# Two gated 3x3 convolutions on one core: the 18 products of the first 12 steps whose results nobody reads are left out

## The chip, the cores and the metric

The kernel runs on one core of a Trainium2 chip. The metric is the device time of one execution in microseconds (us). Several executions are timed; the median stands for the kernel. One execution was also profiled, and all rows below are of that one.

## The reference, cut to what matters

A residual block with two 3x3 convolutions over x of shape (16, 64, 56, 56) in float32. Each convolution is split by input channels: the first 16 channels give yp, the other 48 give yr, and yr is scaled by a gate made of yp.

```python
def qconv_cg(x, w, theta):
    base = x.shape[1] // 4
    yp = conv3x3(x[:, :base], w[:, :base])
    yr = conv3x3(x[:, base:], w[:, base:])
    d = sigmoid(2.0 * (yp - theta[None, :, None, None]))
    return yp + d * yr

h = relu(bn(qconv_cg(x, w_a, theta_a), gamma_a, beta_a, mean_a, var_a))
h = bn(qconv_cg(h, w_b, theta_b), gamma_b, beta_b, mean_b, var_b)
return relu(x + h)
```

## The kernel before, in words

**Rows and tiles.** The 64 input channels are four groups (g = 0 to 3) of 16. Two image rows of opposite parity lie beside each other in the partitions, so a group has 32 partitions and a product of TensorE contracts over the 32 rows of one group. TensorE's array thus works as four row tiles, one for each group; products on different row tiles run beside each other. Group 0 makes yp, groups 1 to 3 add up yr. x and the intermediate h are split into a high and a low part (x_hi, x_lo, h_hi, h_lo), the weights too (w_hi, w_lo); a block of output rows needs 18 products per group: high by high, high by low and low by high weight parts in turn, six taps each (`unit`, lines 502 to 514; the product itself is line 511).

**Steps.** The products are emitted in steps. In a step each group that has work emits one product, in the order g = 1, 2, 3, 0 (lines 519 to 525). `begins` (line 516) says at which step a group starts its next block: group 1 at step 18 times the visit, group 2 six steps later, group 3 twelve steps later (`OFFSET`, line 32); group 0 is without its offset for its first three visits (`EARLY`). So in steps 0 to 5 only groups 1 and 0 have a block, in steps 6 to 11 groups 1, 2 and 0, and from step 12 on all four. Which block a group takes at which visit is set by `TURNS` (line 30): group 1 starts with block 0, group 2 with block 1, group 3 with block 2, and group 0 with block 0.

**The products nobody reads.** Lines 538 to 545 put, at the head of each of the first 12 steps, one more product on the row tile of every group of 2 and 3 that has no block yet: group 2 in steps 0 to 5, group 3 in steps 0 to 11, 18 in all. Each takes weights and x of its group's partitions with 398 columns (`SPARE`) and writes PSUM bank 1 (group 2) or bank 2 (group 3) with start and stop set. The first real product of group 2 in bank 1, and of group 3 in bank 2, starts its sum anew. At step 0 they wait for the same two semaphores (`xhi0_ready`, `whi_ready`) that the first real product waits for at lines 552 and 553.

**What TensorE does ahead of step 0.** Seven products of 128 rows and 512 columns on zeros (line 465, `WARM`), then 12 transposes that bring the weights of the first convolution into their layout (line 457). ScalarE copies the transposed weights to w_hi (line 601), VectorE makes w_lo (line 730).

**What ends the waits near the change.** Block 0's x_hi is cast by VectorE (line 773). Block 1's x_hi is made by ScalarE (`split_hi`, line 621) behind the copies of w_hi and a table load with a first use of Sqrt (line 631). Group 2's first product, at step 6, waits for it (line 555, `xhi_ready`); TensorE takes its products in order, so what is emitted behind that wait waits too.

```python
            for g in (1, 2, 3, 0):
                for visit in range(TOTAL):
                    for u in range(UNITS):
                        steps.setdefault(begins(g, visit) + u, []).append((g, visit, u))
```

Of the kernel before, what the change touches and what calls it, by code (L numbers as in the profile page):

```python
# [23 lines left out]
ROWS = 2 * GR  # L24
BLK, BLK_B = 8, 9
SHORT, SHORT_PAIRS = 7, 2
# [5 lines left out]
OFFSET = (6, 0, 6, 12)  # L32
# [8 lines left out]
def gated_conv_pair_kernel(nc, x, w_a, theta_a, gamma_a, beta_a, mean_a, var_a,  # L41
# [5 lines left out]
    PITCH = W + 1  # L47
# [110 lines left out]
    with ExitStack() as ctx:  # L158
# [64 lines left out]
        whi_ready = sem("whi_ready")  # L223
# [224 lines left out]
        @block.tensor  # L448
        def _(pe):
            def weights(k, c, bank):  # L450

                pe.wait_ge(wpad_ready, 4 + 2 * k + 1 + c)
                pe.wait_ge(wpad_odd_ready, 2 * k + 1 + c)
                for dx in range(TAPS):
                    to = psum[:, bank, dx * P:(dx + 1) * P].rearrange("p (c q) -> p q c", q=2)
                    for mq in range(2):
                        last = pe.transpose(  # L457
                            to[:, mq], w_pad[k][:, 2 * c - mq + 1, dx].rearrange("o i q -> o (i q)"),
                            ident[:])
                last.then_inc(wt_ready, 1)  # L460


            pe.wait_ge(zeros_ready, 1)
            for n in range(WARM):
                mm = pe.matmul(psum[:, 0, :], h_lo[:, 0:P], h_lo[:, 0:BANK], start=True, stop=True)
            mm.then_inc(warm_done, 1)
            pe.wait_ge(ident_ready, 2)
            for c in range(2):
                weights(0, c, 6 + c)
            pe.wait_ge(warm_done, 1)  # L470

            def moving(blk, part, c, dx, g):

                kind, n = blk
                rows = slice(g * ROWS, (g + 1) * ROWS)
                back = 1 - leading(blk)
                if kind == "a":
                    tile = (x_hi, x_lo)[part]
                    parts = a_slots[n]
                    img, s, k = parts[0]  # L480
                    at = back + (s + c) * PITCH + dx
                    if len(parts) == 1:
                        return tile[rows, img % XH_IMGS, at:at + k * PITCH - back]
                    return tile[rows, img % XH_IMGS:img % XH_IMGS + 2, at:at + k * PITCH]
                if kind == "e":
                    return (e_hi, e_lo)[part][rows, c, dx:dx + EDGE * PITCH]
                img, s, k = b_slots(n)
                at = back + ((img % H_IMGS) * SLOTS + s - 1 + c) * PITCH + dx
                return (h_hi, h_lo)[part][rows, at:at + k * PITCH - back]

            def sums(bank, blk):

                kind, n = blk
                to = psum[:, bank, 0:slots_of(blk) * PITCH - 1 + leading(blk)]
                if kind == "a" and len(a_slots[n]) == 2:
                    return to.rearrange("p (i w) -> p i w", i=2)
                return to

            UNITS = 2 * TAPS * 3
            SPARE = SHORT * PITCH - 1  # L500

            def unit(g, b, u):

                kind, n = blk = order[b]
                hi, lo = {"a": (w_hi[0], w_lo[0]), "b": (w_hi[1], w_lo[1]), "e": (w_edge_hi, w_edge_lo)}[kind]
                kind3, tap = divmod(u, 2 * TAPS)
                part, w = ((0, hi), (0, lo), (1, hi))[kind3]
                c, dx = divmod(tap, TAPS)
                bank = YR_BANKS + b % YP_BANKS if g == 0 else b % YR_BANKS
                alone = g == 0  # L510
                return pe.matmul(sums(bank, blk), w[g * ROWS:(g + 1) * ROWS, tap],  # L511
                                 moving(blk, part, c, dx, g),
                                 start=(u == 0 and (alone or g == bank_groups(b)[0])),
                                 stop=(u == UNITS - 1 and (alone or g == bank_groups(b)[-1])))

            def begins(g, visit):
                return UNITS * visit + (0 if g == 0 and visit < EARLY else OFFSET[g])

            steps = {}
# [5 lines that stand above are left out]
            for step in sorted(steps):  # L525
                if step == 24:
                    pe.wait_ge(prmdup_ready, 2)
                    pe.transpose(psum[:, 7, 0:10], prm_dup[:].rearrange("n c q -> n (c q)"),
                                 ident[0:10, 0:10]).then_inc(prmT_ready, 1)
                if step in W_STEPS:  # L530

                    c = W_STEPS.index(step)
                    if c:
                        pe.wait_ge(wlo_ready, 3)
                    else:
                        pe.wait_ge(rvar_ready, 1)
                    weights(1, c, W_BANK)
                for g in (2, 3):
                    if step < OFFSET[g]:

                        if step == 0:
                            pe.wait_ge(xhi0_ready, 1)
                            pe.wait_ge(whi_ready, 1)
                        pe.matmul(psum[:, g - 1, 0:SPARE], w_hi[0][g * ROWS:(g + 1) * ROWS, 0],  # L544
                                  x_hi[g * ROWS:(g + 1) * ROWS, 0, 1:1 + SPARE], start=True, stop=True)
                for g, visit, u in steps[step]:
                    b = visited(g, visit)
                    kind, n = blk = order[b]
                    if u == 0 and g == bank_groups(b)[0]:
                        if kind == "a":  # L550
                            if n == 0:
                                pe.wait_ge(xhi0_ready, 1)
                                pe.wait_ge(whi_ready, 1)
                            else:
                                pe.wait_ge(xhi_ready, chunks_needed(n) - 1)
                        else:
                            pe.wait_ge(hhi_ready, a_needed((kind, n)))
                            if (kind, n) == ("b", 0):
                                pe.wait_ge(hpads_zero, 4)
                            if kind == "e":  # L560
                                pe.wait_ge(edges_ready, 2 * (edge_sources.index(a_needed(blk) - 1) + 1))
                                pe.wait_ge(wedge_ready, 4)
                        if b >= YR_BANKS:
                            pe.wait_ge(gated_ready, b - YR_BANKS + 1)
                    if b == 0 and g == 1 and u == TAPS:
                        pe.wait_ge(whi_ready, 2)
                    if b == 0 and g == 1 and u == 2 * TAPS:
                        pe.wait_ge(wlo_ready, 2)
                    if u == 4 * TAPS and g == bank_groups(b)[0]:
                        if kind == "a":  # L570
                            pe.wait_ge(xlo_ready, chunks_needed(n))
                        else:
                            pe.wait_ge(hlo_ready, 2 * a_needed((kind, n)))
                    if u == 0 and group_before(g, b):

                        pe.wait_ge(visit_done[group_before(g, b)], visits(group_before(g, b), b))
                    if g == 0 and u == 0 and b >= YP_BANKS:

                        pe.wait_ge(gate_ready, b - YP_BANKS + 1)
                        was, m = order[b - YP_BANKS]  # L580
                        if was == "a":
                            pe.wait_ge(za_ready, m + 1)
                        else:
                            pe.wait_ge(zb_ready, second_of[was, m] + 1)

                    if g == 0 and u == 0 and b == 1:
                        pe.wait_ge(wlo_ready, 2)
                    if g == 0 and u == 0 and b == 2:
                        pe.wait_ge(rvar_ready, 1)
                    if u == 0 and b == 4 and g == bank_groups(b)[0]:  # L590
                        pe.wait_ge(whi_ready, 4)
                        pe.wait_ge(wlo_ready, 4)
                    mm = unit(g, b, u)
                    if u == UNITS - 1:
                        mm.then_inc(visit_done[g], 1)
# [292 lines left out]
```

## Time and profile before

| what | value |
|---|---|
| median of 3 runs | 440.07 us (439.25 to 441.33) |
| the profiled execution, its own time | 439.4 us |
| its span, first to last instruction | 437.5 us |
| TensorE busy (matmul) | 427.3 us, 98% of the span, 7826 products |
| ScalarE, VectorE, GpSimd busy | 197.2, 245.1 and 32.2 us |
| mean granted TensorE clock | 0.994 |

The span is 1.9 us shorter than the execution's own time; that remainder lies around the span and belongs to the launch. Busy times are shares of the whole span and say nothing about one stage: the start, in which the change lies, is read from a timeline. The profile models the end of a product, so the distance between two starts on one row tile says more than the duration of one product.

### The profile page before, as it was taken

The page shows a single profiled execution, that of the slowest core. Times are in us where ns is not written, and L with a number is a line of the kernel's source. Part 1 is how long each engine was busy: PE and PEld are TensorE (multiplying, and loading weights), DVE is VectorE, ACT ScalarE, POOL GpSimd, SP SyncE. Part 2 cuts the span into 40 slices and gives each one's busy share as a digit, 9 for nine tenths or more (in the row PEclk, how much of TensorE's full clock was granted, in tenths as well). Part 3 has the DMA queues.
Part 4 walks back from the last instruction along what each step waited for, and adds up shares of the span by engine and source line. Part 5 has one row for each costly group of instructions (what it writes and reads, how often), then busy time and mean ns, then how long its engine had stood idle before and what let it go on. Part 6 is the DMA issues. An engine that isn't in the chain of part 4 may idle for free.

```text
span 437.5 us, 17328 instructions
## 1 busy us (share of the span) xinstructions
PE 427.3 (98%) x7826; PEld 423.9 (97%) x7826; DVE 245.1 (56%) x414; ACT 197.2 (45%) x340; POOL 32.2 (7%) x82
## 2 busy tenths in 40 slices
PE   7999999999999999999999999999999999999992
PEld 6999999999999999999999999999999999999992
DVE  6566546744754862574475476366457457536624
ACT  6755344534534652453353453354345344424223
POOL 6221000000000100000000000011000000000001
PEclk9999999999999999999999999999999999999997
DMA  8920026142426110410523241161622422012044
GB/s 170 190 62 4 3 49 122 35 92 51 88 37 124 25 27 2 99 43 11 124 50 75 49 98 41 37 120 26 121 49 51 76 49 49 3 27 51 14 86 92
DMA packets 119530, 27.57 MB, mean 63 GB/s; under 512 B 119328, under 2 KB 119328, under 8 KB 119456
## 3 DMA queue, kind: packets, MB, share of 16 engines
q1 hardware_dynamic: 117488, 26.09, 29.8%
q8 instruction: 62, 1.02, 1.0%
q10 hardware_dynamic: 1648, 0.36, 0.4%
q14 instruction: 12, 0.10, 0.1%
q0 software_dynamic: 320, 0.00, 0.0%
HBM read 13.60 MB, written 12.85 MB: 60 GB/s over the span
## 4 chain that ended last, share of the span: by engine, by line
PE 96%; ACT 1%; DMA 1%; DVE 0%; ACTq 0%; issue 0%
PE acc L511 96%; DMA early<-in_L_conv_w_a_dram 1%; ACT rows_out L678 0%; PE acc L457 0%; ACT L631 0%; DVE early L718 0%; ACT w_hi L601 0%; ACTq L354 0%; ACT mix L653 0%; ACT z L661 0%; ACT rows_out L676 0%; ACT x_hi L621 0%; ACT probe L631 0%; PE acc L544 0%; ACTq L600 0%
## 5 line engine op out<-in xcount | busy, mean ns | idle before, releaser
L511 PE MATMUL acc<-x_hi,w_hi 32*128 32x456 f32 (+1 forms) x1392 | 278.5, 358 | 0.4 <-ACT x_hi L621 0.4
L511 PE MATMUL acc<-x_lo,w_hi 32*128 32x456 f32 (+1 forms) x1392 | 278.9, 358 | 0.0
L511 PE MATMUL acc<-x_hi,w_lo 32*128 32x456 f32 (+1 forms) x1392 | 278.6, 359 | 0.0
L511 PE MATMUL acc<-h_hi,w_hi 32*128 32x512 f32 x1152 | 263.5, 389 | 0.0
L511 PE MATMUL acc<-h_hi,w_lo 32*128 32x512 f32 x1152 | 263.3, 389 | 0.0
L511 PE MATMUL acc<-h_lo,w_hi 32*128 32x512 f32 x1152 | 263.3, 389 | 0.0
L511 PEld LDWEIGHTS acc<-x_hi,w_lo 32*128 32x128 f32 x1392 | 235.6, 183 | 0.3
L511 PEld LDWEIGHTS acc<-x_lo,w_hi 32*128 32x128 f32 x1392 | 235.7, 183 | 0.1
L511 PEld LDWEIGHTS acc<-x_hi,w_hi 32*128 32x128 f32 x1392 | 234.6, 183 | 1.1 <-ACT x_hi L621 0.8
L511 PEld LDWEIGHTS acc<-h_hi,w_hi 32*128 32x128 f32 x1152 | 200.3, 183 | 0.0
L511 PEld LDWEIGHTS acc<-h_lo,w_hi 32*128 32x128 f32 x1152 | 198.7, 183 | 0.0
L511 PEld LDWEIGHTS acc<-h_hi,w_lo 32*128 32x128 f32 x1152 | 198.7, 183 | 0.0
L653 ACT ACTIVATE mix<-acc,gate_bias 128x448 f32<-128x448 f32 (+2 forms) x108 | 69.6, 644 | 204.3 <-PE acc L511 204.1
L793 DVE TENSOR_TENSOR mix<-mix,acc 128x448 f32<-128x448 f32 (+2 forms) x108 | 68.5, 634 | 88.6 <-PE acc L511 88.4
L812 DVE SCALAR_TENSOR_TENSOR rows_out<-acc,inv,x 128x504 f32<-128x504 f32 x48 | 35.5, 740 | 78.1 <-ACT mix L653 78.1
L678 ACT ACTIVATE rows_out<-rows_out,shift 128x504 f32<-128x504 f32 (+1 forms) x49 | 34.4, 710 | 25.1 <-DVE rows_out L828 25.1
L658 ACT ACTIVATE z<-acc,shift,inv 128x448 f32<-128x448 f32 (+1 forms) x58 | 40.8, 704 | 0.0
L820 DVE SCALAR_TENSOR_TENSOR mix<-mix,inv,z 128x448 f32<-128x448 f32 (+1 forms) x58 | 38.9, 670 | 2.0
L828 DVE SCALAR_TENSOR_TENSOR rows_out<-mix,inv,rows_out 128x504 f32<-128x504 f32 (+1 forms) x50 | 37.2, 744 | 2.3 <-POOL rows_out L446 0.6
L769 DVE TENSOR_TENSOR x_lo<-x,x_hi 128x448 fp32r<-128x448 f32 (+3 forms) x52 | 33.7, 682 | 6.1 <-ACT x_hi L621 6.0
L843 DVE SCALAR_TENSOR_TENSOR h_lo<-mix,h_hi 128x448 fp32r<-128x448 f32 (+2 forms) x64 | 33.2, 569 | 0.1
L439 POOL CAST e_hi<-h_hi 128x57 fp32r<-128x57 f32 (+1 forms) x26 | 8.5, 329 | 324.2 <-ACT h_hi L671 235.5
(78 smaller groups left out, 179.4 us busy)
## 6 DMA issues: line engine op xcount, KB each, us to landing
out_dram<-rows_out SPq DMA_DIRECT2D x95, 126.0 KB, 2.7
x<-in_x_dram SPq DMA_DIRECT2D x28, 392.0 KB, 5.5
x<-in_x_dram SPq DMA_DIRECT2D x2, 294.0 KB, 4.3
x<-in_x_dram SPq DMA_DIRECT2D x2, 280.0 KB, 4.9
early<-in_x_dram SPq DMA_DIRECT2D x4, 112.0 KB, 4.1
out_dram<-rows_out SPq DMA_DIRECT2D x3, 112.0 KB, 2.4
x<-in_x_dram SPq DMA_DIRECT2D x2, 98.0 KB, 3.9
early<-in_L_conv_w_a_dram SPq DMA_DIRECT2D x1, 144.0 KB, 3.1
```

The lines of the kernel that those rows point to most:

```text
L439: nc.gpsimd.tensor_copy(slots(to, img % EDGE, pair), src[:, :, at]).then_inc(edges_ready, 1)
L511: return pe.matmul(sums(bank, blk), w[g * ROWS:(g + 1) * ROWS, tap], moving(blk, part, c, dx, g), start=(u == 0 and (alone or g == bank_gr ...
L653: nc.scalar.activation(mix_rows(b), yp_rows(b), ACT.Sigmoid, scale=ALPHA, bias=gate_bias[:, k:k + 1]).then_inc(gate_ready, 1)
L658: nc.scalar.activation(z_of(n).rearrange("p (s w) -> p s w", w=W), yp_rows(b), ACT.Identity, scale=inv[:, 0:1], bias=shift[:, 0:1]).then_i ...
L678: nc.scalar.activation(out_of(m), out_of(m), ACT.Relu, bias=shift[:, 1:2]).then_inc(out_ready, 1)
L769: nc.vector.tensor_tensor(split_chunk(x_lo, n), x_chunk(n), split_chunk(x_hi, n).bitcast(F32), ALU.subtract).then_inc(xlo_ready, 1)
L793: nc.vector.tensor_tensor(mix_rows(b), mix_rows(b), yr_rows(b), ALU.mult).then_inc(gated_ready, 1)
L812: nc.vector.scalar_tensor_tensor(out_of(m).rearrange("p (s w) -> p s w", w=W), yp_rows(b), inv[:, 1:2], was, ALU.mult, ALU.add).then_inc(z ...
L820: nc.vector.scalar_tensor_tensor(mixed(b), mixed(b), inv[:, 0:1], z_of(n), ALU.mult, ALU.add).then_inc(summed_ready, 1)
L828: nc.vector.scalar_tensor_tensor(out_of(m), mixed(b), inv[:, 1:2], out_of(m), ALU.mult, ALU.add).then_inc(summed_ready, 1)
L843: nc.vector.scalar_tensor_tensor(part[0], part[1], 0.0, part[2], ALU.max, ALU.subtract).then_inc(hlo_ready, 2 // images)
```

## The change

Lines 538 to 545 go, and the constant `SPARE` (line 500) with them. Nothing is added and nothing is moved.

```diff
             UNITS = 2 * TAPS * 3
-            SPARE = SHORT * PITCH - 1
...
                     weights(1, c, W_BANK)
-                for g in (2, 3):
-                    if step < OFFSET[g]:
-
-                        if step == 0:
-                            pe.wait_ge(xhi0_ready, 1)
-                            pe.wait_ge(whi_ready, 1)
-                        pe.matmul(psum[:, g - 1, 0:SPARE], w_hi[0][g * ROWS:(g + 1) * ROWS, 0],
-                                  x_hi[g * ROWS:(g + 1) * ROWS, 0, 1:1 + SPARE], start=True, stop=True)
                 for g, visit, u in steps[step]:
                     b = visited(g, visit)
```

## Rows read from the trace of the kernel before

**Rows 1.** The page's chain that ended last: shares of the span by engine.

```profile
PE 96%; ACT 1%; DMA 1%; DVE 0%; ACTq 0%; issue 0%
```

**Rows 2.** TensorE's waits, whole span: total us, times, longest us.

```profile
PE acc L511 <- ACT x_hi L621: 0.4, 1, 0.4
PE acc L544 <- ACT w_hi L601: 0.4, 1, 0.4
```

**Rows 3.** The critical chain in order of time: start us, us, what.

```profile
5.73 0.87 ACT w_hi L601 x2
...
6.62 1.28 ACT L631
...
8.12 0.43 ACT x_hi L621
...
18.22 410.25 PE acc L511 x6757
```

**Rows 4.** All instructions of line 544: ns min/median/max, first and last start.

```profile
L544 PE MATMUL acc<-x_hi,w_hi x18: 336/342/445, 6.4 to 9.4; 32*128 32x398 f32 x18
```

**Rows 5.** Timeline of TensorE around the change: start us, us, what.

```profile
6.37 0.58 PE L544 MATMUL acc<-x_hi,w_hi 32*128 32x398 f32 x2 [0.36 <-ACT w_hi L601]
6.66 0.45 PE L511 MATMUL acc<-x_hi,w_hi 32*128 32x398 f32 x2
...
7.84 0.34 PE L511 MATMUL acc<-x_hi,w_lo 32*128 32x398 f32 x1
8.59 0.45 PE L511 MATMUL acc<-x_hi,w_hi 32*128 32x398 f32 x1 [0.41 <-ACT x_hi L621]
...
8.60 0.45 PE L544 MATMUL acc<-x_hi,w_hi 32*128 32x398 f32 x1
...
8.88 0.34 PE L544 MATMUL acc<-x_hi,w_hi 32*128 32x398 f32 x1
...
9.44 0.34 PE L544 MATMUL acc<-x_hi,w_hi 32*128 32x398 f32 x1
9.61 0.33 PE L511 MATMUL acc<-x_hi,w_hi 32*128 32x398 f32 x1
```

**Rows 6.** Timeline of VectorE around the change.

```profile
6.25 1.02 DVE L730 TENSOR_TENSOR w_lo<-acc,w_hi 128x384 fp32r<-128x384 f32 x2 [1.17 <-ACT w_hi L601]
```

**Rows 7.** Timeline of TensorE in mid-kernel, four row tiles at work.

```profile
199.69 0.39 PE L511 MATMUL acc<-h_hi,w_lo 32*128 32x512 f32 x1
...
199.84 0.36 PE L511 MATMUL acc<-x_hi,w_hi 32*128 32x456 f32 x1
...
200.46 0.36 PE L511 MATMUL acc<-x_hi,w_hi 32*128 32x456 f32 x1
...
200.62 0.39 PE L511 MATMUL acc<-h_hi,w_lo 32*128 32x512 f32 x1
```

**Rows 8.** Timeline of TensorE's last products, one row tile at work.

```profile
428.30 1.39 PE L511 MATMUL acc<-e_lo,w_edge_hi 32*128 32x456 f32 x6
```

**Rows 9.** Timeline of TensorE ahead of step 0.

```profile
1.31 3.36 PE L465 MATMUL acc<-h_lo 128*128 128x512 f32 x7 [1.31 <-POOL h_lo L400]
...
1.91 1.48 PE L465 MATMUL acc<-h_lo 128*128 128x512 f32 x3
...
4.04 0.63 PE L465 MATMUL acc<-h_lo 128*128 128x512 f32 x1
4.92 1.08 PE L457 MATMUL acc<-ident,early 64*128 64x64 f32 x12 [0.25 <-DVE early L718]
```

**Rows 10.** Stretches: length, busy PE, PEld, DVE, ACT, POOL (x); PEclk, DMA, GB/s.

```profile
1.50:2.00 0.50, 0.50 (x2) 0.40 (x3) 0.41 (x5) 0.23 (x1) 0.23 (x1) 1.00 0.00 0
...
8.00:8.50 0.50, 0.18 (x3) 0.00 (x0) 0.00 (x0) 0.50 (x3) 0.49 (x1) 1.00 0.80 192
...
429.00:430.00 1.00, 0.69 (x4) 0.28 (x2) 0.96 (x2) 1.00 (x3) 0.17 (x1) 1.00 0.00 0
...
431.00:432.00 1.00, 0.00 (x0) 0.00 (x0) 0.64 (x1) 0.55 (x1) 0.26 (x1) 0.97 0.33 74
432.00:433.00 1.00, 0.00 (x0) 0.00 (x0) 0.05 (x1) 0.58 (x1) 0.00 (x0) 0.50 0.89 191
```

## The prediction

> **What bounds the kernel now.** I read the page's chain first: 96% of the span is TensorE, so a microsecond taken from TensorE's own work, or from a wait of TensorE, is a microsecond of the kernel [rows 1]. The list of TensorE's waits comes next, because it tells where that is not so. Two of its few waits touch the change: 0.4 us ahead of the first product of line 544, which ends with ScalarE's first copy of w_hi, and 0.4 us ahead of a product of line 511, which ends with ScalarE's x_hi [rows 2]. The chain in order of time shows the same from the other side: up to 8.59 us it runs through ScalarE (the w_hi copies, a table load of 1.28 us, then x_hi from 8.12 on), and from 18.22 us it is one piece of 410.25 us of TensorE [rows 3]. So the start has two regimes. Until 8.59 us TensorE is ahead of ScalarE and its own work is covered; behind 8.59 us nothing covers it.
>
> The 18 products of the change lie on both sides of that line. The view of line 544 finds all 18, from 6.4 to 9.4 us [rows 4]. By the steps, two belong to each of steps 0 to 5 and one to each of steps 6 to 11. The timeline places them: steps 0 to 5 begin at 6.37, and of step 6 group 1's product still runs at 7.84; then nothing starts until 8.59, when group 2's first product gets its x_hi [rows 5]. So 13 products (12, and that of step 6, which is emitted ahead of the wait) start before the wait ends, and 5 (steps 7 to 11, at 8.60 to 9.44) behind it.
>
> **The 13 ahead of the wait: 0.** At step 0 the first products of line 544 start at 6.37 and the first of line 511 at 6.66 [rows 5]. Without them group 1's product can take the place at 6.37, so steps 0 to 5 may run up to 6.66 - 6.37 = 0.29 us earlier. Their semaphores are the same, so the wait for w_hi moves to line 511 and doesn't vanish. The second w_hi copy, at 5.73 + 0.87 = 6.60, and w_lo, at 6.25 + 1.02 = 7.27, are there ahead of their use at steps 3 and 6 [rows 3, 6]. But what follows is step 6's wait for x_hi, which ScalarE finishes at 8.12 + 0.43 = 8.55 in a chain (w_hi, table load, x_hi) in which none of these products occurs [rows 3]. TensorE's gap of 0.41 us grows to at most 0.70, and 8.59 stays 8.59. The cover is ScalarE's table load. Without it, up to 0.29 us of gain would show.
>
> **The 5 behind the wait: 0 to 0.23 us, taken as 0.** These stand beside real products of groups 1, 2 and 0 on other row tiles. Do they slow them? Take a step's price with four row tiles and with one. With four at work, 456 columns go from 199.84 to 200.46 in three steps, 0.207 us each [rows 7]. At the very end group 3 is alone: six products of 456 columns in 1.39 us; less the 0.36 us that the last one takes, five distances of 0.206 us [rows 8]. One alone takes as long as one of four, so a product that is left out beside others saves nothing. The lower end is 5 x 0.001 = 0.005 us of gain. For the upper end I let the array be shared, each product costing a fourth of a step: behind the wait a step of 398 columns takes (9.61 - 8.88)/4 = 0.183 us [rows 5], a fourth is 0.046, times 5 is 0.23 us. I take the lower end, because rows 7 and 8 are the very comparison that the change makes.
>
> The Trainium skill (TensorE: Matmul & The Clock Gate, section "Measured speedup vs the span model") has tiles start side by side at about 4 ns for each further one; as an estimate by that page the 5 products give 5 x 4 ns = 0.02 us. The trace's 0.206 against 0.207 shows less than that.
>
> **The sum.** 0 for the 13, 0 for the 5. The profiled execution stays at 439.4 us (437.5 span and 1.9 around it), which is 0.7 below the median of the runs, 440.07, as runs go here. A forecast for the median is 440.07 - 0.03, so 440.0 us. About 0.5% (2.2 us) is what a measurement of this kernel can tell from no change. The runs alone spread from 439.25 to 441.33.
>
> **Rival S, slower: the clock falls in the thinner start.** Place: TensorE between the transposes, which end at 4.92 + 1.08 = 6.00 [rows 9], and 8.59. Before, it had four row tiles at work for most of 6.37 to 8.18, and a gap of 0.41; after, two row tiles for at most that long, and a gap of up to 0.70. That the clock has two levels here can be seen at both ends. The seven products at the start are (4.04 - 1.91)/5 = 0.426 us apart for 512 columns [rows 9], against (200.62 - 199.69)/4 = 0.233 us in mid-kernel [rows 7]: 512 columns in 0.426 us is 1.2 GHz, while 0.233 us, which also holds what is not streaming, needs 2.4 GHz. (The PEclk column says 1.00 at 1.5 to 2 us too [rows 10]; the spacing decides.) At the end PEclk stays 1.00 to about 431.9 and is 0.50 from 432 on, some 2.2 us behind the end of the last product, 428.30 + 1.39 = 429.69 [rows 8, 10].
>
> Price: at the low level a step of 398 columns takes 0.183 x 0.426/0.233 = 0.335 us, so 0.152/0.335 = 45% of each low microsecond is lost, and behind 8.59 nothing gives it back. How long it would be low is bounded by the first time: TensorE began at 1.31, was low at least until 4.04 + 0.43 = 4.47 and high from 6.66 on at the latest [rows 5, 9]. That is 3.2 to 5.4 us, or 1.4 to 2.4 us lost: 441.5 to 442.5 us, with 441.9 in the middle. It decides from the point where two row tiles with a 0.70 us gap are treated as the quiet end was, and not as the four tiles before. For it: the end shows that one tile for 1.4 us and then 2.2 us of nothing do lower the clock. Against it: the new gap is a third of that 2.2 us, at least two row tiles work on either side of it, and the gap of 0.41 us before left the clock at 1.00, with steps of 0.183 us from 8.88 on [rows 5, 10].
>
> The Trainium skill (TensorE: Matmul & The Clock Gate, section "What's actually happening") says that the slow clock is the default and recent activity releases it; by that rule taking work away ahead of a stall speaks against the change, and it would give the time of S. The trace agrees on the two levels and on the fall behind the last product; whether two of four row tiles keep the release no row shows.
>
> **Rival F, a little faster: the array is shared after all.** Then 0.23 us behind the wait is gained, and 439.8 us is the time. Rows 7 and 8 speak against it, and the difference could not be told from none. If in addition ScalarE's chain were late for another reason that these products cause, up to 0.29 us more would come, 439.5 us; no row shows such a tie.
>
> **That the change does nothing at all** is hardly open: the 18 records of line 544 have no reader, and they go. That is the forecast's own mechanism.
>
> **How the numbers follow.** The forecast has 0.62, S 0.28, F 0.06; 0.04 is left for what I have not seen (a second fall of the clock or a late weight). Forecast and F lie within 0.5%, up to 442.3 and down to 437.9. Of S's 1.4 to 2.4 us only the top reaches 2.2 us, and a run's spread of a microsecond can carry the rest over, so I give S 0.13 slower and 0.15 same. With the remainder: slower by over 0.5% 0.15, within 0.5% 0.81, faster 0.04. The range reaches down to the lowest run of before, 439.2, and up to nearly all of S, 442.4. The forecast's own range is 439.2 to 441.4, the spread of the runs.
>
> **What would show it.** In the profile after, line 544 has no rows; line 511's first product starts near 6.37 behind ScalarE's w_hi; the gap ahead of group 2's first product is 0.4 to 0.7 us and still ends at 8.59 with ScalarE's x_hi; steps 7 to 11 stay 0.183 us apart; the last product still ends near 429.7. The forecast is wrong if distances of about 0.33 us appear anywhere between 6.4 and 14 us (S: the later transposes then start 1.4 to 2.4 us later than before), or if the x_hi of ScalarE moves.

## The result, and the profile after

| what | before | after |
|---|---|---|
| median, same session, 22 runs each | 439.74 us (439.08 to 441.52) | 441.3 us (440.54 to 442.2) |
| ratio after to before, 95% interval | | 1.0031 [1.0021, 1.0041] |
| the profiled execution | 439.4 us | 440.84 us |
| its span | 437.5 us | 438.9 us |
| mean granted TensorE clock | 0.994 | 0.988 |

The kernel is slower by 0.31%, 0.9 to 1.8 us (a ratio is one of means, near 441.4 and 440.1 here, and not of medians). That is less than the 0.5% that the prediction took as the bound of what can be told, but with 22 runs a side it can be told. The forecast, no change, did not happen. One thing is needed to read the numbers: the runs of both kernels fall into groups, by when TensorE's clock rises at the start (see the last experiments), so the median of few runs depends on the mix (the 440.07 us of the first three runs became 439.74 with 22).

First the page of the kernel after: its head, the row of TensorE and the shares of the chain that ended last.

```profile
span 438.9 us, 17290 instructions
...
PE 428.6 (98%) x7808; PEld 425.1 (97%) x7808; DVE 245.0 (56%) x414; ACT 197.2 (45%) x340; POOL 32.1 (7%) x82
...
PE 97%; ACT 1%; ACTq 0%; POOL 0%; issue 0%; POOLq 0%
```

18 products fewer (7826 - 18 = 7808) and yet TensorE is busy 1.3 us longer (428.6 against 427.3). Work went and busy time came: the products that are left must take longer somewhere. The critical chain in order of time (start us, us, what) says where.

```profile
6.48 1.28 ACT L622
...
7.98 0.43 ACT x_hi L612
...
8.45 8.09 PE acc L510 x126
...
19.61 410.25 PE acc L510 x6762
```

Against [rows 3]: the last piece of TensorE lasts 410.25 us in both, to the hundredth, so everything from there on is untouched. It begins at 19.61 where it began at 18.22: +1.39 us, the whole difference of the spans (438.9 - 437.5 = 1.4). Up to the wait for x_hi nothing is lost either: that wait ends at 8.45, 0.14 us earlier than the 8.59 of before, because TensorE's transposes and ScalarE's chain behind them ran that much earlier in this execution (the table load at 6.48, before at 6.62). So 1.39 + 0.14 = 1.53 us is lost between 8.45 and 19.61. TensorE's timeline (start us, us, what) shows the place; its last row is the end of the kernel, for later.

```profile
6.23 1.35 PE L510 MATMUL acc<-x_hi,w_hi 32*128 32x398 f32 x12 [0.36 <-ACT w_hi L592]
7.40 0.34 PE L510 MATMUL acc<-x_hi,w_lo 32*128 32x398 f32 x1
8.45 0.57 PE L510 MATMUL acc<-x_hi,w_hi 32*128 32x398 f32 x1 [0.71 <-ACT x_hi L612]
...
8.83 0.53 PE L510 MATMUL acc<-x_hi,w_hi 32*128 32x398 f32 x1
...
9.16 0.53 PE L510 MATMUL acc<-x_hi,w_hi 32*128 32x398 f32 x1
...
12.10 0.34 PE L510 MATMUL acc<-x_lo,w_hi 32*128 32x398 f32 x1
...
12.28 0.34 PE L510 MATMUL acc<-x_lo,w_hi 32*128 32x398 f32 x1
...
429.68 1.39 PE L510 MATMUL acc<-e_lo,w_edge_hi 32*128 32x456 f32 x6
```

Until 7.74 the products are as before (0.34 us each). Behind the wait one takes 0.53 us, and the steps are 9.16 - 8.83 = 0.33 us apart; from 12.10 on they are 0.18 apart again. Before, steps of 398 columns were 0.183 us apart behind the wait [rows 5]. The stretches with the granted clock confirm it (length; busy PE, PEld, DVE, ACT, POOL, each with its instructions; PEclk, DMA share, GB/s).

```profile
8.00:8.50 0.50, 0.05 (x3) 0.05 (x3) 0.07 (x1) 0.50 (x2) 0.42 (x1) 1.00 0.65 114
8.50:9.00 0.50, 0.50 (x6) 0.50 (x9) 0.50 (x2) 0.50 (x2) 0.00 (x0) 0.61 1.12 195
9.00:9.50 0.50, 0.50 (x12) 0.50 (x8) 0.50 (x2) 0.24 (x1) 0.00 (x0) 0.50 1.26 206
...
12.00:12.50 0.50, 0.50 (x19) 0.50 (x16) 0.00 (x0) 0.00 (x0) 0.00 (x0) 0.97 1.26 218
12.50:13.00 0.50, 0.50 (x17) 0.50 (x12) 0.00 (x0) 0.00 (x0) 0.00 (x0) 1.00 1.34 238
...
431.00:432.00 1.00, 0.07 (x1) 0.00 (x0) 1.00 (x2) 1.00 (x3) 0.78 (x1) 0.93 0.00 0
```

PEclk falls from 1.00 to 0.50, 1.2 GHz, inside 8.5 to 9.0 and is back inside 12.0 to 12.5. A mean of 0.61 over 0.5 us is 0.11 us at 1.00 and the rest at 0.50: the fall is at 8.61, the rise (0.97) at 12.03. That is 3.42 us, and at 45% lost of each low microsecond (the prediction's own price) 3.42 x 0.45 = 1.54 us. It is the 1.53 us of the chain. **Rival S happened**, with the price that stood in the prediction.

### The profile page after: what moved, and what is told of

It is laid out like the page before. It is cut to its first block, busy times and chain, and to the rows that moved or that the text cites. A ratio compares the mean times of both kernels' runs of the same rounds, so it can differ in the third digit from the quotient of the medians.

```text
span 438.9 us, 17290 instructions
## 1 busy us (share of the span) xinstructions
PE 428.6 (98%) x7808; PEld 425.1 (97%) x7808; DVE 245.0 (56%) x414; ACT 197.2 (45%) x340; POOL 32.1 (7%) x82
## 4 chain that ended last, share of the span: by engine, by line
PE 97%; ACT 1%; ACTq 0%; POOL 0%; issue 0%; POOLq 0%
PE acc L510 96%; PE acc L465 1%; ACT rows_out L669 0%; PE acc L457 0%; ACT L622 0%; ACT w_hi L592 0%; ACTq L354 0%; ACT mix L644 0%; ACT z L652 0%; ACT rows_out L667 0%; POOL h_lo L400 0%; ACT x_hi L612 0%; ACT probe L622 0%; ACTq L591 0%; POOLq L868 0%
```

## Experiments

After this profile three theories stood. **C**: the clock falls because less of the array is at work ahead of the wait; the twelve products of steps 0 to 5 held it. **G**: the clock falls because the gap of TensorE in front of x_hi grew from 0.41 to 0.71 us. **B**: the six products of steps 6 to 11, mostly behind the wait, are what counts. A run carries the mark of a fall in its mean granted clock: it is 0.988 in every profile with a stretch at 0.50 near the start and 0.992 or more in those without. I count runs at 0.988 or below as marked. Of 90 runs of the kernel before that ran beside the experiments (a further one, at 1092.19 us, is left out), none has the mark; of 31 runs of the kernel after (here and below) about half do, and none is under 440.5 us. Diffs are against the kernel before unless said otherwise.

### Which of the products: e1 and e2

```diff
-                    if step < OFFSET[g]:
+                    if step < 6:
```

> Kept: the 12 unread products of steps 0 to 5 (groups 2 and 3). Left out: the 6 of group 3 in steps 6 to 11. Theory C (the clock falls because only two of four row tiles work ahead of the stall at 8.5 us): the granted clock stays 1.00 up to the end and the median is that of the kernel before, 439.7 us, ratio 1.000 within 0.001. Rival G (the gap of 0.71 instead of 0.41 us lets it fall): the gap is as before, about 0.4 us or some 0.1 more since the product of step 6 is gone, so also about 439.7; G is told apart by e4. Rival B (the products behind the stall are what holds the clock): as the changed kernel, ratio 1.003, about 441.2 us, with some 3.4 us at 0.50.

e1 keeps the twelve unread products of steps 0 to 5 and leaves out the six of steps 6 to 11.

```diff
-                    if step < OFFSET[g]:
+                    if g == 3 and 6 <= step < 12:
```

> Kept: the 6 unread products of group 3 in steps 6 to 11. Left out: the 12 of steps 0 to 5. Theory C: as the changed kernel, ratio 1.003 (441.1 us), the profile with a stretch of about 3.4 us at 0.50 from about 8.6 us on and step distances of 0.33 us. Rival G: the same, as the gap is 0.6 to 0.7 us. Rival B: as the kernel before, 439.7 us, clock 1.00.

e2 is the other half: it keeps the six and leaves out the twelve. Measured, beside 28 runs of the kernel before (439.45 median): e1 1.0006 [0.9992, 1.0021], with 4 of 12 runs under 439.3 us and one with the mark (its profile is of another run, at 441.39 us, that started low); e2 1.0038 [1.0023, 1.0054], no run under 441.0, three of 7 with the mark. e2's stretches, same columns, then three rows of TensorE's timeline:

```profile
8.50:9.00 0.50, 0.21 (x4) 0.21 (x8) 0.23 (x1) 0.50 (x2) 0.11 (x1) 1.00 0.99 184
9.00:9.50 0.50, 0.50 (x12) 0.50 (x12) 0.50 (x2) 0.50 (x3) 0.00 (x0) 0.56 1.21 242
...
12.00:12.50 0.50, 0.50 (x12) 0.50 (x12) 0.00 (x0) 0.00 (x0) 0.00 (x0) 0.53 1.27 240
```

```profile
9.40 0.53 PE L511 MATMUL acc<-x_hi,w_hi 32*128 32x398 f32 x1
...
9.41 0.53 PE L544 MATMUL acc<-x_hi,w_hi 32*128 32x398 f32 x1
...
9.73 0.53 PE L511 MATMUL acc<-x_hi,w_hi 32*128 32x398 f32 x1
```

The fall comes with four row tiles at work behind the wait (three real products and e2's unread one, line 544), as it does in the kernel after with three. So the loss belongs to the twelve products ahead of it, which by the prediction were covered, and B falls. The six behind cost and bring nothing that can be told, as forecast: at the low clock a step with four row tiles takes 9.73 - 9.40 = 0.33 us, and one with three in the kernel after 0.33 as well. The one marked run of e1 says that the twelve do not hold the clock in every run.

### The gap or the work: e3 and e4

e3 leaves out all 18 unread products and puts twelve others on the row tiles that have a block (1 and 0), after the real ones of steps 0 to 5, so that TensorE still has two row tiles at work but for longer:

```diff
-                for g in (2, 3):
...
+                if step < 6:
+                    for g in (1, 0):
+                        pe.matmul(psum[:, 3 + (g == 0), 0:SPARE], w_hi[0][g * ROWS:(g + 1) * ROWS, 0],
+                                  x_hi[g * ROWS:(g + 1) * ROWS, 0, 1:1 + SPARE], start=True, stop=True)
```

> The 18 unread products are left out and 12 others put in, as many as those of steps 0 to 5, but on the row tiles of groups 1 and 0, which have work already: each of steps 0 to 5 takes twice as long (0.37 us), two row tiles work from 6.3 to about 8.5 us, and hardly a gap is left. Theory C in its strict form (how many row tiles work at once counts): the clock falls all the same, ratio 1.003. Theory C in its loose form (the sum of the array's work ahead of the stall counts): as before, ratio 1.000. Rival G: no gap, the clock stays, ratio 1.000 or a little below.

e4 keeps all 18 and makes the gap longer, by three more operations on ScalarE ahead of x_hi:

```diff
-        probe = sb("probe", [P, 2])
+        probe = sb("probe", [P, 5])
...
             nc.scalar.activation(probe[:, 0:1], probe[:, 0:1], ACT.Sqrt)
+            for n in range(2, 5):
+                nc.scalar.activation(probe[:, n:n + 1], probe[:, n:n + 1], ACT.Sqrt)
```

> The kernel before with all 18 products, and three more small ScalarE instructions of some 0.11 us each ahead of its first x_hi, so that the gap of 0.41 us becomes about 0.75 us, longer than that of the changed kernel (0.71). Theory C: the clock stays at 1.00, and the time grows by the delay alone, 0.3 us, to 440.0 us, ratio 1.0008. Rival G: the clock falls as in the changed kernel, 0.3 + 1.5 us, ratio 1.004.

e3: 1.0039 [1.0018, 1.0059]. TensorE's timeline in its profile, then the stretches:

```profile
8.53 0.37 PE L590 MATMUL acc<-x_hi,w_hi 32*128 32x398 f32 x2
...
8.66 0.46 PE L511 MATMUL acc<-x_hi,w_hi 32*128 32x398 f32 x1
```

```profile
8.00:8.50 0.50, 0.50 (x8) 0.50 (x6) 0.00 (x0) 0.50 (x2) 0.42 (x1) 1.00 0.72 197
8.50:9.00 0.50, 0.50 (x12) 0.50 (x11) 0.36 (x1) 0.50 (x3) 0.00 (x0) 0.96 0.85 146
9.00:9.50 0.50, 0.50 (x9) 0.50 (x6) 0.50 (x2) 0.45 (x2) 0.00 (x0) 0.50 1.33 264
```

There is no gap at all here: TensorE is busy 0.50 of 0.50 from 8.0 on and no wait for x_hi is left, and still PEclk goes to 0.50, at 8.96. Three runs carry the mark (440.69 to 440.93), two stayed at 439.35 and 439.62; the five others, at 442.3 to 442.8 without the mark, are probably runs with the low start that the last experiments show.

e4: 1.0019 [1.0004, 1.0035], and one mark in 12. Its ScalarE timeline shows that the edit did what it should:

```profile
8.27 0.37 ACT L633 ACTIVATE probe<-probe 128x1 f32<-128x1 f32 x3
8.54 1.35 ACT L621 ACTIVATE x_hi<-x 128x392 fp32r<-128x392 f32 x3
```

x_hi starts 8.54 - 8.27 = 0.27 us later than it would without them, and the lowest of e4's runs is as much later, 439.40 against 439.11 of the kernel before beside it. Its profile (441.68 us) is a low start, as by their times the three other runs at 441.7 to 441.8, and these make most of the ratio. What counts is the runs that start high: three, at 439.4 to 439.8, kept the clock with a gap that by this sum is about 0.41 + 0.27 = 0.68 us (no profile caught one of them), as long as that of the kernel after, of which no run came under 440.5; one, at 441.33, has the mark. e9, below, shows such a gap in a profile with the clock kept. So the gap alone doesn't lower the clock, and in e3 two row tiles do so without one: G falls as the cause, C stands. That a longer gap adds to it, the one mark leaves possible.

### How much of the array: e5, e6 and e7

Is it the number of row tiles, or the sum of their work? e5 gives three tiles all the way, e6 four tiles for half as long; both have 12 unread products.

```diff
-                    if step < OFFSET[g]:
+                    if g == 3 and step < 12:
```

> Kept: the 12 unread products of group 3 (steps 0 to 11). Left out: the 6 of group 2 in steps 0 to 5, so that three row tiles work ahead of the stall instead of four or two. Theory C (the share of the array at work ahead of the stall decides) leaves open where between two and four it turns: either as the kernel before (439.5 us, no run with a mean clock of 0.988 or lower) or as the changed one (441.1 us, every second run at 0.988 or lower); a mean in between, some runs falling and some not, would say that three tiles are near the edge. A rival that any two groups' missing products cost a share each gives half the loss in every run: 440.3 us in all of them.

```diff
-                    if step < OFFSET[g]:
+                    if step < 3 or (g == 3 and 6 <= step < 12):
```

> Kept: the unread products of steps 0 to 2 on groups 2 and 3 (6 of 12), and those of group 3 in steps 6 to 11. Left out: those of steps 3 to 5. So four row tiles work for the first half of the time ahead of the stall and two for the second: the same sum of work as with three tiles (18 real and unread products less than four tiles all the time). If the sum of the array's work counts, the same as with three tiles; if what lies just ahead of the stall counts, as the changed kernel (441.1 us).

e5: 1.0019 [1.0005, 1.0033]. Eight of 12 runs carry the mark, one more is at 0.991, and none is under 440 us. Its stretches:

```profile
8.00:8.50 0.50, 0.14 (x4) 0.14 (x8) 0.16 (x1) 0.50 (x2) 0.25 (x1) 0.94 0.84 126
8.50:9.00 0.50, 0.50 (x8) 0.50 (x12) 0.50 (x2) 0.50 (x2) 0.00 (x0) 0.50 1.31 220
```

The clock falls at 8.44, though three row tiles worked. e6: 1.0020 [1.0006, 1.0033], but from another mixture: two of 12 runs with the mark, five between 440.2 and 440.5 with 0.994 or 0.995, one at 439.35; one more is at 0.991. The same ratio from different runs decides nothing between the number of tiles and the sum of their work, and e3 points at the number alone only weakly (as many products as before on two tiles, three falls in five). That stays open.

e7 leaves out the 18 and puts three unread products on the whole array, one behind each of steps 1, 3 and 5:

```diff
-                for g in (2, 3):
...
+                if step in (1, 3, 5):
+                    pe.matmul(psum[:, 3, 0:SPARE], w_hi[0][:, 0], x_hi[:, 0, 1:1 + SPARE], start=True, stop=True)
```

> All 18 unread products are left out; instead three products that nobody reads, of 128 rows by 398 columns, which take the whole array, stand behind steps 1, 3 and 5. They fill as many row tiles for as long as the 12 did (3 x 4 = 12), by 3 instructions and in time that is a gap in the changed kernel (3 x 0.18 = 0.55 of 0.71 us). Theory C: the clock doesn't fall, most runs are as the kernel before, 439.2 to 440.5 us, and none or few have a mean clock of 0.988; where the clock is still low from the start, up to 0.6 us is lost since the three then take 0.33 each. Rival (the very 18 products on their row tiles are needed, or it is a matter of row tiles alternating): as the changed kernel, 441.1 us or above.

1.0096 [1.0078, 1.0114], the slowest of all. TensorE's timeline:

```profile
6.48 1.03 PE L511 MATMUL acc<-x_hi,w_hi 32*128 32x398 f32 x4
7.44 0.70 PE L589 MATMUL acc<-x_hi,w_hi 128*128 128x398 f32 x1
8.07 1.03 PE L511 MATMUL acc<-x_hi,w_hi 32*128 32x398 f32 x4
9.03 0.70 PE L589 MATMUL acc<-x_hi,w_hi 128*128 128x398 f32 x1
```

Two steps and one full product take 8.07 - 6.48 = 1.59 us; three steps at the low clock would be 3 x 0.33 = 1.0. Going from row tiles to the whole array and back costs about 0.3 us each way, so step 6 is late by itself. One of its six runs has the mark (442.92), too few to say anything of the clock. The Trainium skill (TensorEngine Tiling (Array Packing), section "Key Properties") states that a change of tiling mode drains TensorE; the 0.63 us from the full product to the next step's start (8.07 - 7.44), against 0.33 between steps, agree.

The kernel after, unchanged, ran beside these:

> The changed kernel again, on the chip and in the hour of the others. Theory C: 441.1 to 441.6 us on the median, about half of the runs with a mean clock of 0.988 or lower (the fall after 8.5 us), the others with 0.992 or 0.993 and 441.5 to 442.1 us, whose clock is low from the start until later than in the kernel before; no run below 440.4 us.

1.0044 [1.0027, 1.0061], four marks in six runs.

### Taking the stall away instead: e8 and e9

If TensorE didn't wait for x_hi at all, would the change be free? e8 makes block 1's x_hi ahead of the table load, in the kernel after; e9 does so in the kernel before.

```diff
+            split_hi(1)
             act.wait_ge(probe_zero, 1)
             nc.scalar.activation(probe[:, 0:1], probe[:, 0:1], ACT.Sqrt)
-            for n in range(1, SOON):
+            for n in range(2, SOON):
                 split_hi(n)
```

> The changed kernel, with ScalarE's first x_hi moved ahead of its table load, so that the stall ahead of group 2's first product loses up to 1.4 us of what it waits for. If the x it needs has landed by 6.5 us, the stall of 0.71 us goes and step 6 follows step 5; otherwise the landing sets its end. Theory C (thin work and a stall together let the clock fall): without the stall few or no runs have a mean clock of 0.988, and these are at 438.5 to 439.0 us, below the kernel before. Rival (two row tiles alone suffice, as with the twelve products on two tiles): falls as in the changed kernel, 440.4 to 441.4 us.

> The kernel before with the same move of ScalarE's first x_hi. With four row tiles the clock stays in any theory; only the stall of 0.41 us goes: 439.0 us where the clock is high from the start, 0.3 to 0.4 below the kernel before, ratio 0.999; nothing gained in the runs whose clock is low during steps 0 to 5, since these have no stall.

e8: 1.0028 [1.0014, 1.0041], five marks in 12. e9: 1.0003 [0.9991, 1.0015], none. The edit missed its aim; ScalarE's timeline, e8 first, then e9:

```profile
8.00 0.53 ACT L612 ACTIVATE x_hi<-x 128x392 fp32r<-128x392 f32 x1 [0.97 <-DMA x<-in_x_dram]
```

```profile
8.08 0.53 ACT L621 ACTIVATE x_hi<-x 128x392 fp32r<-128x392 f32 x1 [1.64 <-DMA x<-in_x_dram]
```

x_hi now waits for the transfer of x itself, and ends at 8.53 and 8.61, where it ended at 7.98 + 0.43 = 8.41 and 8.12 + 0.43 = 8.55: no earlier. The prediction called the table load the cover of the 13 products; right beside it stands the landing of x, so by these rows hardly any of the 0.29 us would have shown without the load. With the load behind it, the next x_hi is late instead, in e9's TensorE timeline; two stretches follow:

```profile
8.66 0.45 PE L511 MATMUL acc<-x_hi,w_hi 32*128 32x398 f32 x1 [0.66 <-ACT x_hi L621]
...
10.60 0.44 PE L511 MATMUL acc<-x_hi,w_hi 32*128 32x398 f32 x1 [0.40 <-ACT x_hi L621]
```

```profile
8.50:9.00 0.50, 0.34 (x8) 0.34 (x12) 0.35 (x1) 0.48 (x2) 0.00 (x0) 1.00 0.46 72
9.00:9.50 0.50, 0.50 (x17) 0.50 (x12) 0.22 (x1) 0.50 (x1) 0.00 (x0) 1.00 0.70 152
```

This settles more of G than e4 does: with all 18 products in place the gap is 0.66 us here, near the 0.71 of the kernel after, and PEclk stays 1.00 behind it. With one edit in both, e8 without the 18 products has five marks in 12 runs and e9 with them none.

e9's 12 runs lie within 0.33 us (439.97 to 440.30), where the kernel before spread over 2.5 us beside it (439.06 to 441.56). A likely reason is that its two waits end by ScalarE, so that what TensorE loses at a low clock ahead of them is lost in time that it would have waited; its one profile started high and doesn't show it.

### Other work in the gap: e10

If C holds, other unread work on all four row tiles should hold the clock as well as the twelve products did. e10 leaves out the 18 and, ahead of step 6's real products, emits three rounds of unread products on four tiles, in the time in which TensorE waits for x_hi:

```diff
-                for g in (2, 3):
...
+                if step == 6:
+                    for n in range(3):
+                        for g in (1, 2, 3, 0):
+                            pe.matmul(psum[:, (4, 3, 1, 2)[g], 0:SPARE], w_hi[0][g * ROWS:(g + 1) * ROWS, 0],
+                                      x_hi[g * ROWS:(g + 1) * ROWS, 0, 1:1 + SPARE], start=True, stop=True)
```

> The 18 unread products are left out; 12 unread products, three on each of the four row tiles, stand between step 5 and step 6 instead, in what is a gap of 0.71 us in the changed kernel (3 x 0.183 = 0.55 us at the high clock). Steps 0 to 5 stay thin, with two row tiles. If the array's work ahead of the fall counts (theory C with the sum): few or no runs at a mean clock of 0.988, and runs at 439.1 to 439.5 us come back. If four row tiles are needed all through steps 0 to 5, or those very products: as the changed kernel, half of the runs at 0.988 and none below 440.4 us. Where the clock is low from the start, the three steps take 1.0 us instead of 0.55 and push step 6 back, so these runs may be 0.5 to 0.9 us above the changed kernel's 441.6.

1.0019 [0.9998, 1.0041]. No run of 12 carries the mark: four are at 439.0 to 439.43, a place that no run of the kernel after reached, and eight at 441.9 to 442.2. Its profile is one of these eight, and a low start, as by their times the other seven probably are; the chain in order of time shows what the three rounds cost there:

```profile
8.58 0.14 PE acc L541 x2
8.73 0.19 PE acc L511 x2
8.91 0.33 PE acc L541 x4
9.25 0.30 PE acc L511
9.55 0.36 PE acc L541 x3
```

At 0.33 us a round, three rounds are 1.0 us of TensorE on the chain; at 0.18 us a round their 0.55 us would fit into a gap of 0.71. So in the four runs that started high the work in the gap held the clock, as C has it; that it fills the gap is not enough, for e3 has none and fell. It gives nothing that the kernel before has not. No kernel tried here was faster than that one; the lowest ratio is e9's, 1.0003.

### Single profiles: the runs that start low

> The changed kernel, one more profile. Theory C: it shows one of two courses, either the fall to 0.50 for some 3.4 us behind 8 us (span near 439.1 us), or steps of 0.33 us from the start until later than 11 us with no granted 0.50 on record (span near 440.1 us).

> The kernel before, one more profile. Theory C: no stretch at 0.50 ahead of 430 us; either steps of 0.183 us from the start (span near 437.4 us) or steps of 0.33 us until some moment between 9.5 and 13 us (span 438.3 to 439.6 us).

> The changed kernel, one more profile, for its runs near 442 us: if one is caught, the clock is low from the start and rises later than 13 us, or it rises, falls and rises again.

> The changed kernel, one more profile, with the same expectation as the one before it.

> The kernel before, one more profile, for its runs near 440.3 us: if one is caught, steps of 0.33 us from the start until about 11 us, and no granted 0.50 ahead of 430 us.

All five are unchanged kernels, and all five profiles show another course: the clock has not risen yet when step 0 begins. The kernel before, at 441.52 us (TensorE's timeline of r_before):

```profile
6.50 0.83 PE L544 MATMUL acc<-x_hi,w_hi 32*128 32x398 f32 x2
...
12.07 0.53 PE L511 MATMUL acc<-x_hi,w_lo 32*128 32x398 f32 x1
...
13.20 0.34 PE L511 MATMUL acc<-x_lo,w_hi 32*128 32x398 f32 x1
```

The first pair takes 0.83 us where it took 0.58 [rows 5], and products take 0.53 us until about 12.9. PEclk reads 1.00 all the while, as it did in the warm-up [rows 10]: the spacing decides. In r_before2, at 440.44 us, the rise comes at about 10.3:

```profile
9.77 0.53 PE L511 MATMUL acc<-x_hi,w_hi 32*128 32x398 f32 x1
...
10.44 0.36 PE L511 MATMUL acc<-x_hi,w_hi 32*128 32x398 f32 x1
...
10.64 0.34 PE L511 MATMUL acc<-x_hi,w_hi 32*128 32x398 f32 x1
```

The kernel after has these courses too, r_after2 for one, with its first twelve products in 2.35 us where they took 1.35 above:

```profile
6.42 2.35 PE L510 MATMUL acc<-x_hi,w_hi 32*128 32x398 f32 x12
```

In every one of these the last piece of the chain is 410.25 us again, and its start alone tells the time:

```
profile      run us   clock high from     410.25 us piece from
before       439.40   ahead of step 0     18.22
r_before2    440.44   about 10.3          19.25
r_before     441.52   about 12.9          20.34
after        440.84   (low 8.61 to 12.03) 19.61
r_after      441.07   (low 8.96 to 12.4)  19.89
r_after4     441.40   about 12.6          20.21
r_after2     441.63   about 13.0          20.45
r_after3     441.74   about 13.4          20.55
```

So the groups of runs are groups of the clock's first rise. Of the 90 runs of before, 44 lie at 439.1 to 439.6, 31 at 439.9 to 440.5 and 15 at 441.4 to 441.6, near the times of these three profiles. The change hits the first group: by times and marks its runs get the fall and stand at 440.7 to 441.1 (two profiles show it). Whether it also delays the rise in the low starts (12.6 to 13.4 in three profiles of after, 10.3 and 12.9 in two of before) is likely from the times (of 31 runs of after only two, at 440.54 and 440.73 without the mark, can have risen as early as r_before2), but five profiles don't show it. Some runs of after at 442.0 to 442.2 with a mean clock of 0.986 were not caught in a profile; what happens in them is open.

## Why the prediction was wrong

**The 13 ahead of the wait: right as far as it went.** The first product of a real block took the place at 6.23, the wait for w_hi moved to it and stayed 0.36 us, and the gap ahead of x_hi became 0.71 us, forecast at most 0.70. None of it moved x_hi, and the wait ended at 8.45 where 8.59 "stays", the difference being the chain that ran 0.14 us earlier. As work, they cost nothing.

**The 5 behind the wait: not contradicted.** e1 without the six of steps 6 to 11 is 1.0006 [0.9992, 1.0021], which is too wide to tell 0 from the 0.23 us of the upper end. The step spacings speak for 0, at the low clock only: 0.33 us with four row tiles (e2) and with three (the kernel after).

**Rival S: the mechanism, the place and the price were right, the chance was not.** Forecast: low for 3.2 to 5.4 us, 1.4 to 2.4 us lost; measured 3.42 and 1.53. Its time, 441.5 to 442.5, added the loss to the median, 440.07; the fall hits the runs that start high, near 439.3, and so gives 440.7 to 441.1. The step that failed is its "Against it": "the new gap is a third of that 2.2 us, at least two row tiles work on either side of it". Both halves are wrong. The gap is no measure: e3 falls without one, and e9 stays up with one of 0.66 us. Even the 2.2 us of the tail was no measure. In the kernel after the last products end at 429.68 + 1.39 = 431.07 (the last row of its timeline), and PEclk, at 0.93 from 431 to 432, falls at 431.86, 0.8 us behind them; before, it was 2.2 us. The clock fell at 431.9 in both, though the products ended 1.4 us apart, so the quiet time ahead of a fall, read from one execution, bounds nothing. And "at least two row tiles work" was read as a guard, but the clock went with two of four at work (the kernel after, e3), and with three (e5). The Trainium skill (TensorE: Matmul & The Clock Gate, section "Loop structure matters more than you think") has matmuls that stay back to back keep the clock, and long waits lower it; e3, back to back on two row tiles across 8.5 us, lost it, so for products on a part of the array the measurement differs. What the Trainium skill says on the same page in the section "What's actually happening", and the prediction quoted against the change, agrees with the fall and with e10: less activity, and the clock went.

**The runs' spread.** "The runs alone spread from 439.25 to 441.33" stood as noise of the measurement. It was the clock's first rise, early enough or 1 or 2 us dear (18.22, 19.25, 20.34). Read so, it would have said that the clock is not settled in the start of this kernel, and that this is worth as much as all of S.

**The sum.** 440.0 against 441.3: the term missing is the 1.53 us of S in the runs that start high and, probably, later places for runs that start low, which are about half of the runs. **Of the range**, 439.2 to 442.4, S made the upper end, and the result lies in it.

## What to carry to other kernels

Work that nobody reads and nothing waits for can still be worth its place: where TensorE runs on row tiles, look at how many of them are busy ahead of a stall before calling idle ones free. A product covered by a wait costs nothing as work, and still the clock went without it; test its removal with the granted clock and the step spacing, over many runs. And where runs of one kernel fall into groups, find what separates them (here where one long untouched piece of the chain begins) before taking the spread for noise.

## What the runs showed that was not expected

- With three of four row tiles at work ahead of the wait the clock fell in eight of 12 runs (e5); with four, in none of 90 of the kernel before and in one of 12 each of e1 and e4, by their marks.
- The clock's first rise is not tied to the kernel: ahead of 6.4 us, at 10.3 or at 12.9 in three executions of the same program, though TensorE's first product starts at 1.31 [rows 9].
- The fall moves too: 8.61 in the first profile after, 8.96 in another, 8.44 in e5, 9.06 in e2.
- The PEclk column reads 1.00 ahead of the first recorded change even where steps are 0.33 us apart; it can show a fall, not a late first rise.
- One full-array product between steps of row tiles costs about 0.6 us more than its own columns at the low clock (e7).
